# A 6-layer local-attention transformer behind a recurrence on one core: mask written by ScalarE, token transpose ahead of the output projection, activation tables fetched by one-column operations, input copy of the feed-forward one step later

## What is computed

```python
# recurrence
n = layernorm(x)
h = tanh(h @ A.T + (n @ B.T)[t]);  y[t] = h @ C.T
r = x + (layernorm(y + n) * gamma + beta)
# six times, from x = layernorm(r); the output is r + the last x
t = shift_tokens(x); q, k, v = split(t @ Wqkv)
q = l2norm(q) * q_scale; k = l2norm(k) * k_scale          # then rotary tables, with scales
sim = q @ k_look.T * 8;  sim = where(mask, -max, sim);  p = softmax(sim)
x = (p @ v_look) @ Wo + x
t = shift_tokens(x); n = layernorm(t) * g + b
x = ((n @ W1a + b1a) * gelu(n @ W1g + b1g)) @ W2 + b2 + x
```

## Time and profile before

| | |
|---|---|
| median of three runs | 3563.22 us |
| the profiled execution | 3561.33 us |
| its span in the profile | 3559.5 us |
| granted TensorE clock | 1.00 in nearly all slices of the page; the mean is 0.995 |
| busy: TensorE / VectorE / GpSimd / ScalarE | 96 / 79 / 64 / 61% |
| first projection of the layers | 403.6 us |
| last q projection of the layers | 3471.3 us |

### The profile page before, as it was taken

One profiled execution on the slowest core, in us unless ns is written; L12 is line 12 of the kernel. 1 busy time (PEld: TensorE's weight loads), 2 busy tenths in 40 slices (PEclk: granted clock), 3 DMA queues, 4 the chain that ended last, 5 costly groups with the idle time before them and its releaser, 6 DMA issues. The chain is left out here.

```text
span 3559.5 us, 101336 instructions
## 1 busy us (share of the span) xinstructions
PE 3403.3 (96%) x42643; PEld 2170.8 (61%) x42643; DVE 2822.8 (79%) x4367; ACT 2155.9 (61%) x4211; POOL 2263.3 (64%) x1363
## 2 busy tenths in 40 slices
PE   8999699999999999999999999999999999999996
PEld 4555366666666666666666666666666666666664
DVE  3444498888888888888888888888888888888883
ACT  2222256666666666666666666666666666666664
POOL 0000267777676777777777777677677676777773
PEclk9999899999999999999999999999999999999999
DMA  2000000100000100001000001000001000000000
GB/s 70 1 1 1 4 11 11 32 11 11 11 12 13 34 11 11 8 17 34 11 8 11 11 17 31 11 11 11 8 17 35 11 11 8 11 17 13 14 11 13
DMA packets 62282, 52.54 MB, mean 15 GB/s; under 512 B 11527, under 2 KB 59397, under 8 KB 61829
## 3 DMA queue, kind: packets, MB, share of 16 engines
q1 hardware_dynamic: 61828, 46.05, 4.9%
HBM read 43.93 MB, written 2.10 MB: 13 GB/s over the span
## 5 line engine op out<-in xcount | busy, mean ns | idle before, releaser
L431 POOL TENSOR_TENSOR cosp<-cosp,rr 128x1024 f32<-128x1024 f32 x384 | 722.6, 1903 | 636.8 <-DVE rr L922 636.6
L441 POOL TENSOR_TENSOR cosp<-cosp,sinp 128x1024 f32<-128x1024 f32 x384 | 907.7, 2369 | 101.1 <-DVE sinp L901 98.0
L623 PEld LDWEIGHTS ps<-px,w_vo 128*128 128x128 f32 x6144 | 700.5, 192 | 224.3 <-DVE sh L994 219.6
L623 PE MATMUL ps<-px,w_vo 128*128 128x128 f32 x6144 | 735.7, 278 | 66.8 <-DVE sh L994 55.6
L527 PE MATMUL ps<-w_qk,xs 128*128 128x512 f32 x1536 | 749.5, 611 | 10.0 <-ACT sq L735 5.1
L735 ACT ACTIVATE sq<-ps 128x1024 f32<-128x1024 f32 x384 | 392.3, 1021 | 402.5 <-DVE sinp L901 402.5
L898 DVE TENSOR_TENSOR cosp<-ps,tab 128x1024 f32<-128x1024 f32 x384 | 469.5, 1223 | 203.2 <-PE ps L527 202.0
L907 DVE TENSOR_REDUCE ss<-sq 128x16 f32<-128x1024 f32 x384 | 455.5, 1186 | 94.9 <-ACT sq L735 94.9
L527 PEld LDWEIGHTS ps<-w_qk,xs 128*128 128x128 f32 x1536 | 263.3, 191 | 343.6 <-issue 341.7
L683 PE MATMUL ps<-pT,xtm 32*128 32x512 f32 x3072 | 458.6, 616 | 9.8 <-DVE pT L973 4.7
L901 DVE TENSOR_TENSOR sinp<-ps,tab 128x1024 f32<-128x1024 f32 x384 | 466.6, 1215 | 0.0
(11 more groups left out here) (106 smaller groups left out, 4412.5 us busy)
## 6 DMA issues: line engine op xcount, KB each, us to landing
tab<-in_tab SPq DMA_DIRECT2D x96, 128.0 KB, 2.0
qks<-in_scales SPq DMA_DIRECT2D x96, 128.0 KB, 3.2
w_qk<-in_L_ffn_Wqkv SPq DMA_DIRECT2D x12, 512.0 KB, 7.1
w_v<-in_wv_t SPq DMA_DIRECT2D x6, 512.0 KB, 8.8
w_o<-in_L_ffn_Wo SPq DMA_DIRECT2D x6, 512.0 KB, 10.3
x<-in_L_attn_x SPq DMA_DIRECT2D x16, 128.0 KB, 3.3
out<-w_v SPq DMA_DIRECT2D x16, 128.0 KB, 2.5
w<-in_L_ffn_W SPq DMA_DIRECT2D x6, 341.0 KB
```

Source lines behind the costliest of these rows:

```text
L431: eng.tensor_tensor(v, v, rr[:, B % 2, HEADS * i:HEADS * i + HEADS].unsqueeze(2).to_broadcast([P, HEADS, DH]), ALU.mult).then_inc(rot_read ...
L441: eng.tensor_tensor(cosp[:, A % 2, i, :], cosp[:, A % 2, i, :], sinp[:, i, :], ALU.add).then_inc(rot_added, 1)
L623: t = eng.matmul(S0, w_vo[:, i // HP, i % HP, :], px[:, i, :], start=i == 0, stop=i == HEADS - 1)
```

## The change

- `S` gets its mask by a ScalarE copy of the bf16 mask (128x1024, into two PSUM banks) from the second tile on, placed behind `xtm`, ahead of the q copies, after `centered` of the tile before; the scores wait for `mask_written`. The two mask matmuls stay for the first tile only.
- The token transpose goes ahead of the output projection, into bank 4 (`X`), once two of the three px copies are out. The output projection writes bank 7 (`Y`) and no longer waits for `centered`. The turn of k, which writes these banks, waits for `y_added` and `xt_evac`; so do a layer's weight products.
- Two one-column activations on a new tile `warm`: gelu between the q and k copies of step G, exp between the feed-forward and the root guess of step G.
- The copy `xc` moves from the end of step G to step N, between the mask and the q copies.
- Prologue: input chunk 0 is fetched first, the first normalisation waits for it alone; `layernorm` uses `bn_stats`/`bn_aggr` and a two-scalar `tensor_scalar` per 128 columns. The last chunk's `post` is split: its first layer norm runs inside VectorE's step 0 behind the rotary products of q, the rest behind those of k; the transpose and the copy of its result move into step 1, where TensorE waits for `x_updated` of all chunks ahead of the turns.

```diff
-def layernorm(eng, step, src, dst, c, t4, bits):
+def layernorm(eng, step, src, dst, stat, aggr, t4, bits):
+    for j in range(TB):
+        step.issue(eng.bn_stats(stat[:, j, :], src[:, j, :]))
+    step.settle()
+    for j in range(TB):
+        step.issue(eng.bn_aggr(aggr[:, j, :], stat[:, j, :]))
...
+    for j in range(TB):
+        step.issue(eng.tensor_scalar(dst[:, j, :], src[:, j, :], aggr[:, j, 0:1], r[:, j:j + 1], ALU.subtract, ALU.mult))
...
+        Y = G(3)[:, 0:P]
+        X = G(0)[:, 0:P]
...
+            load_x(0)
+            eng.dma_start(ident[:, :], a["ident"]).then_inc(ident_in, 16)
...
             outputs(NC - 1)
-            turn_input(NC - 1)
...
+                if s == 1:
+                    turn_input(NC - 1)
+                    eng.wait_ge(x_updated, NC)
                 if tile(C):
-                    eng.wait_ge(centered, C + 1)
+                    after(eng, xt_evac, C)
+                    after(eng, px_evac, 3 * E + 2)
+                    eng.transpose(X, xs[:, C % ROUND, :], ident[:, :]).then_inc(xt_done, 1)
                 if tile(E):
...
-                        t = eng.matmul(S0, w_vo[:, i // HP, i % HP, :], px[:, i, :], start=i == 0, stop=i == HEADS - 1)
+                        t = eng.matmul(Y, w_vo[:, i // HP, i % HP, :], px[:, i, :], start=i == 0, stop=i == HEADS - 1)
                     t.then_inc(y_done, 1)
-                if tile(C):
-                    after(eng, xt_evac, C)
-                    eng.transpose(S1, xs[:, C % ROUND, :], ident[:, :]).then_inc(xt_done, 1)
                 L = layer_of(s)
                 if L is not None:
...
+                    after(eng, y_added, E + 1)
+                    eng.wait_ge(xt_evac, C + 1)
...
+                if tile(E):
+                    eng.wait_ge(y_added, E + 1)
+                if tile(C):
+                    eng.wait_ge(xt_evac, C + 1)
                 if tile(B):
                     eng.wait_ge(rot_ready, 2 * B + 2)
                     turn(B, 1, K_BANKS)
...
-                    w = window(B)
-                    for h2 in range(2):
-                        eng.matmul(ps[:, 2 + h2, :].rearrange("p (h k) -> p h k", k=DH), ident_bf[:, :],
-                                   mask[:, DH * w:DH * w + DH].unsqueeze(1).to_broadcast([P, HP, DH]), start=True, stop=False, skip_group_check=True)
+                    if B == 0:
+                        for h2 in range(2):
+                            eng.matmul(ps[:, 2 + h2, :].rearrange("p (h k) -> p h k", k=DH), ident_bf[:, :],
+                                       mask[:, 0:DH].unsqueeze(1).to_broadcast([P, HP, DH]), start=True, stop=False, skip_group_check=True)
+                    after(eng, mask_written, B)
                     eng.wait_ge(turn_evac, 4 * B + 4)
...
+                if tile(B) and B:
+                    w = window(B)
+                    eng.wait_ge(centered, B)
+                    eng.copy(S, mask[:, DH * w:DH * w + DH].unsqueeze(1).to_broadcast([P, HEADS, DH])).then_inc(mask_written, 1)
+                T = turn_of(s, 7)
+                if T is not None:
+                    eng.wait_ge(y_added, ROUND * (T + 1))
+                    after(eng, rows_done, T)
+                    shifted(xc[:, :].rearrange("p (b t) -> p b t", b=BATCH), xb, slice(0, BATCH), turn_cols(T), turn_cols_before(T), xc_ready)
...
+                    if turn_of(s, 10) is not None:
+                        eng.activation(warm[:, 1:2], warm[:, 0:1], ACT.Gelu)
                     for u, k in enumerate(K_BANKS):
...
                 ffn(s)
+                if turn_of(s, 10) is not None:
+                    eng.activation(warm[:, 1:2], warm[:, 0:1], ACT.Exp)
...
-                T = turn_of(s, 6)
-                if T is not None:
-                    eng.wait_ge(y_added, ROUND * (T + 1))
-                    after(eng, rows_done, T)
-                    shifted(xc[:, :].rearrange("p (b t) -> p b t", b=BATCH), xb, slice(0, BATCH), turn_cols(T), turn_cols_before(T), xc_ready)
...
                     rope(A, 0)
+                if s == 0:
+                    post_norm(last)
...
                     rope(A, 1)
+                if s == 0:
+                    post_input(NC - 1, last)
```

More of the change, by code:

```diff
@@ L312, in _, with load_x @@
         def _(eng):
[L313 to L319 removed]
+            def load_x(c):
                 for r in range(2):
```

105 lines of the change are left out of this document (56 added, 49 removed).

## The result

The changed kernel takes 3484.43 us (median of four runs, 3477.18 to 3489.47), the kernel before in the same comparison 3563.43 us: a ratio of 0.9773, 95% interval [0.9761, 0.9785]. It is faster by 2.3%. I had forecast 3428 with a range of 3400 to 3478, so the direction was right and the time was outside the range, 6 us above its end. The profiled execution took 3489.47 us, span 3487.7; my sum made for it was 3426, so 63 us of the promised 135 did not come.

A forecast was written before the change was run, and what follows sets the result against it. TensorE's order of work and its waits were taken as the bound, VectorE close behind. Savings 120 + 8 - 10 + 5.4 + 12 = 135 us took the profiled 3561.3 to 3426, median 3428; range 3400 to 3478.

The forecast's parts named there:

- The parts of a turn: Four steps that 43 turns repeat: N 15.3, V 14.13, F 16.05, G 15.74 us, together 61.2, 2.8 less than before.
- The prologue: Before the layers: earlier fetch of chunk 0 and a shorter `layernorm` bring the first tokens 5.4 us sooner (3.5 to 7).
- rival (c): Step G: the table loads are not moved, G keeps its length less 0.5 us; 3440 us, chance 0.05.
- the missing drain: Rival from the skill's notes: each table load adds about 1.38 us, nearly the whole gain goes; 3540 us, chance 0.04.
- Part 2: Mask ahead of the scores: TensorE loses 0.53 us a step, ScalarE gains a copy taken as 1.02 us.
- Parts 3 and 4: Table loads moved in G, a gain of 0.74 us for G; `xc`, 1.25 us, into N, which gains 1.1.
- A layer's first step: Weight products wait for `y_added` and `xtm`: a gain of 0.74 us becomes a loss of 0.9; 10 us in all.
- The join: From last post work to step 1's k projection: work of step 0 runs beside it, 12 us sooner (9 to 13).
- The lighter steps: Ten steps before the turns and the last with tiles, less feed-forward: some 14 steps at 0.6 us, 8 us gained.
- The drain: The kernel's end holds the same chain as before: a change of 0 us (-2 to 2).
- (a): Rival, half given back: semaphore latencies eat the small spare times at the turn of k and ScalarE; 3480 us, chance 0.18.
- (e): Rival, slower: the mask copy makes ScalarE the bound, from 2.1 us a copy; about 3615 us at 2.5, chance 0.04.

The follow-up runs named there:

- e7_join_undone: The changed kernel with the last chunk's normalisation, input and transposes ahead of the layers' loop again, as before the change; 3485.3 us.
- e5_vo_late: The changed kernel with a layer's 16 weight products moved behind the k projection and ScalarE's four copies of them behind those of qT; 3463.8 us.

## Why the prediction missed

**What was right.** The parts of a turn: N 15.35 for 15.3, V 14.29 for 14.13, F 16.11 for 16.05, G 15.53 for 15.74, together 61.28 for 61.2. The mask copy, 1.04 for 1.02, and that the median V and F carry it free (the k copies still end 0.97 and 2.27 us ahead of the scores). That F is held by VectorE: its k projection waits 0.27 us for the square. The prologue: the first chunk's product starts at 11.47, 5.8 us sooner for 5.4. Of the table loads the worth (15 us, 12 by rival (c)) and the missing drain.

**What was wrong**, against the 63 us that are missing in the profiled execution:

1. *No term for TensorE's supply of instructions*: 28.2 us inside the scores and 4.7 in `p @ tokens`, on the page, against 2.9 of "issue" before (2.5 of it at the output projection): 30 us. Part 2 reads "TensorE loses 0.53 us a step" from the two mask products as pure gain. They were two long instructions ahead of 256 short ones, and they kept 0.44 us more between the end of the k copies and the burst. Parts 3 and 4 let the mask copy, the table load and `xc` make the k copies later in G and N, and priced that at nothing, as the scores' start does not end those steps. But the late fetches of instructions come behind the k copies: these ended 0.99 and 2.27 us ahead of the scores of N and G before, and 0.19 and 1.07 after, and 22 of the 28 us in the scores are in these two steps. Gaps in one burst of ten don't show in the median step, so a sum made from one turn can't have them.
2. *"A layer's first step pays"*, with 0.9 us: it measured 2.72 at full clock (22.70 against 19.98, of it 0.99 a gap in the scores) and 4.07 on average. `y_added` was ready at t = 8.35 (925.45, I had 8.00), the products began at 8.61, ScalarE's copies at 9.81 and not 9.3, and the k projection at 12.85, in the kernel before at 10.24. I let that step keep its gain at the start and the mask's 0.53, though all of it comes ahead of one chain that was later by 2.6. And TensorE's standing still for 2.9 and 1.3 us in it was followed in four of five by a fall of the granted clock from 1.00 to 0.80 to 0.86 of the step, from 2.4 GHz to 1.2 for a part of it; in e5_vo_late, without the 2.9 us, none of the five has a fall. With the first layer step (23.53 for 21.3) this is 5 x 3.2 + 2.3 = 18 us. Moving the products behind the k projection gave 20.6 us back.
3. *The join*, 12 us: at the k projection of step 1 the whole prologue and join were 14.2 us sooner and not 17.4, of which 14.2 - 5.8 = 8.4 are left for the join (undoing the join alone, e7_join_undone, moves that projection by 5.7; the other 2.7 I did not isolate); two steps on it was 4.5, and in the whole time 1. Work that is done sooner at a place where the next chain (the first layer step, at a mean clock of 0.78) is later is lost again.
4. *The lighter steps*, 8 us: from the third step to the first w2 product 159.6 us against 159.7 before, with 3.0 us of gaps in between. I credited steps with less feed-forward work with a part of the gain of others, and no row bore it out.

Without what is counted twice these are 30, 18, 3 (of the join, as its loss in the first layer step is in point 2) and 3 (of the lighter steps, as their gaps are in point 1); 43 turns of 61.28 for 61.2 add 3. That is 57 of 63. The drain has 3 more: I had put it at 0, and from the last q projection to the end of the span it took 91.5 us (3396.2 to 3487.7) against 88.2 before, with the clock at its lower level for 16 us of it against 7; what is cause there no run tells. The last 3 us I can't place; the lower clock outside the layers' steps is a candidate that no run isolates. None of the rivals was what happened: (a) named the size, 3480, by luck, with the wrong mechanism; the added waits of the turn of k cost nothing in the steps. The range ended at 3478, 2 us below the time of (a), though it was said to hold most of (a). (e) is refuted by the copy's 1.04 us. What I had named as proof of an error, a turn above 62.5, did not occur in the median (61.28) or the mean (62.1): the test looked at the steps that I had priced, and the error was outside them.

## What to carry over

A long burst of short instructions needs time between the last wait ahead of it and its start: before taking work from an engine that is 96% busy, look at which instructions let its stream catch up, and at which copies that it waits for move towards the burst. Check by the "issue" time inside the burst and by the mean beside the median of the steps, and see whether such idle times lie 256 records apart and behind a fetch. What is put ahead of a rare step (here a layer's weights) is worth a timeline of its own, as its price includes the clock's. And when a copy's cover moves, so does its cost: the split scores had lost the products that hid the k copies.

## What the runs showed of the hardware

- TensorE stands still inside a burst of 256 records (128 products and their weight loads), issued in 1.41 us, for up to 2.8 us, at a place fixed in its instruction stream: the 193rd or 194th record of each block of 256 in 258 of 258 cases. Kernels with nearly the same stream stall behind the same records.
- TensorE's instructions come in fetches of 16 KB, one per 256 records, of 0.88 to 1.68 us each in the changed kernel. TensorE stands still when such a fetch starts less than about 2.3 us before its block is needed, and goes on 1.25 to 1.56 us after it has landed.
- 1.04 us more of ScalarE ahead of copies that the burst waits for raises the sum of these gaps from 14.7 to 24.1 us, with TensorE's stream unchanged. The late fetches start 1.0 to 1.2 us after the last of these copies in 16 of 19 gaps. What starts a fetch is open.
- A table load takes 1.28 us with and without work behind it, and the next operation starts 0.01 us later; the Trainium skill, "ScalarE: Activation LUTs", section "What ACT_TABLE_LOAD costs", has a drain of about 1.38 us that no run here shows.
- In the steady part, 450 to 3400 us, the granted clock stayed at 1.00 in the kernel before; in the changed one it was at its lower level for 47.8 us, behind gaps and in layer steps, and in the one with the weight products late and the mask on TensorE for none.
